# Two token tiles of the feed-forward input gated and quantised during the last state-space step, and the last batch's expert slots computed after its first shared column

## The chip, the cores and the metric

The kernel runs on one core of a Trainium2 chip. TensorE (PE) does matrix products and transposes into PSUM banks, VectorE (DVE), ScalarE (ACT) and GpSimd (POOL) do elementwise work, and the SyncE queue (SP) issues most transfers. Each engine takes its own instructions in order and waits on semaphores for the others. The metric is the device time of one execution in microseconds, as the median of several runs.

## The reference, cut to what matters

Four sequences of 512 tokens with 512 channels pass through two layers. Layer 0 is a gated linear attention and a mixture of experts (16 experts, 6 chosen for each token, 2 shared). Layer 1 is a state-space mixer (four chunks of 128 tokens in this kernel) and a feed-forward block whose inputs are quantised in blocks of 32. Each of the four blocks reads the running sum through a sigmoid gate and a ratio tensor that hang on the condition.

```python
# _bi_wkv, the gate in front of each block
base = sigmoid(r) * (num / maximum(den, 1e-08))
# state-space mixer, its last steps
Y = Y + x_heads * D_param[:, None]
Y = Y.reshape(Bsz, L, D_INNER) * silu(z)
return rmsnorm(Y) @ fq4(W_out).T
# feed-forward
def _mx_dequant(t):
    blocks = t.reshape(rows, feat // 32, 32)
    scales = maximum(max(abs(blocks)) / 448.0, 1e-30)
    q = (blocks / scales).astype(float8_e4m3fn).astype(float32)
    return (q * scales).reshape(rows, feat)
gate = _mx_dequant(x2d) @ _mx_dequant(gate_w).T
up = _mx_dequant(x2d) @ _mx_dequant(up_w).T
out = _mx_dequant(silu(gate) * up) @ _mx_dequant(down_w).T
# the whole
x = x + L0_attn(L0_cond(x, ...)); x = x + L0_ffn(L0_cond2(x, ...))
x = x + L1_attn(L1_cond(x, ...)); x = x + L1_ffn(L1_cond2(x, ...))
```

## The kernel before

The program has three parts, one after the other. **Layer 0's first part** (0 to about 1262 us) takes the four batches `b` in turn: attention, then `route_and_share`. There PE computes the router's logits and then six shared columns `j` (`ST = 6`): a gate and an up product of 512 columns (L927), and the down product of the column before (L914), each four products (eight records in a trace). DVE ranks the experts in `route`, sends the mask by `m_mask`, then multiplies gate and up of each column (L2021, `m_prod`). At `j == 1` PE makes the prefix sums over the mask (L932, L933, `m_pref`), and after column `j == 2` DVE turns them into slots (`place`, L1944 to L1955, `m_slot`); in the last batch it goes on with `tile_tables` (the expert tiles' tables, `e_tab`) and `pads(0)`, `pads(1)`. On `m_slot` POOL writes the token numbers to their slots with 24 indirect transfers (L1587, `ids_put`). When the last batch's have landed, SP (`first_tiles`, L635) loads the first tiles' token numbers and expert weights, POOL gathers their rows (L1599), and PE starts the **expert tiles** with `expert_x(0)` (L964), which also needs `x1b`, the sum over the shared columns that DVE makes after the last of them (L2038).

**The expert tiles** (63 of 256 slots, to about 2320 us) are followed by **layer 1**, four batches of about 430 us. A batch has projections (L1080), four state-space steps `k` and 16 feed-forward steps `i` (four blocks `ib` of 512 hidden channels by four token tiles `t`).

A state-space step goes: PE broadcasts decays (L1090), DVE subtracts (`differences`, L2225), ACT exponentiates (L1509), DVE masks (`masked`, L2231), PE multiplies (`diagonal`, L1099) and reads the state (L1157, `s_yo`), DVE sums up y (L2259 to L2270, `s_y`), ACT takes its root mean square (L1531, L1533, `s_yss`), DVE the reciprocal (L2281, `s_yr`), ACT scales (`normalise`, L1513), PE transposes (L1107), ACT copies out (L1518), and PE projects in two halves (`out_project`, L1121, `s_out`). Step `k` holds the projection of tile `k - 1`; the last tile's stands behind the loop. DVE adds a projected tile to the running sum (`residual_tile`, L2217, `x3_ready`), and in the last step it does so for tile 2 before it waits for `s_yss`.

Behind the last projection come, for each token tile, ACT's sigmoid (L1538, `sig3`), DVE's product with the ratio R[3] (L2288, `h_tile`), PE's transpose to bank 7 (`x_transpose`, L1180, `f_tx`), DVE's quantisation (`quantise_x`, L1656 to L1666 and L2296 to L2302, `f_qx`), PE's transpose back (`xq_transpose`, L1191, `f_tq`) and ACT's copy to `xqT` (L1543, `f_xT`). Then step `i` can begin: a gate product (L1226), an up product (L1232, `f_gu`), ACT's silu (L1548), DVE's product (L2310, `f_mul`) and quantisation, PE's transposes (L1206) and, once a block, the down products (L1213). Tiles 0 and 1 are quantised ahead of the loop and tiles 2 and 3 inside of it, after DVE's steps 0 and 1. DVE's part in the order before:

```python
dve.reciprocal(ss[:, 2:3], ss[:, 1:2]).then_inc(s_yr.sem, 1)
for k in range(NT):
    if k == NT - 1:
        residual_tile(k)
    ...                      # wait for sig3, h = sigmoid * R[3], h_tile
quantise_x(0)
quantise_x(1)
for i in range(FB * NT):
    ...                      # product, quantise; after i = 0, 1: quantise_x(i + 2)
```

For the next batch POOL gathers expert outputs (`collect(b + 1)`, L1609) from `f_vx` of tile 0 on, and DVE weighs them (`weigh`, L2109, L2111) from step 5 on.

## Time and profile before

| | |
|---|---|
| median of 3 runs | 4135.53 us (4132.06 to 4138.08) |
| the profiled execution | 4128.88 us, of which its span 4127.0 us |
| PE busy | 3569.0 us (86%) |
| DVE busy | 2611.4 us (63%) |
| ACT busy | 1194.5 us (29%) |
| POOL busy | 522.4 us (13%) |
| TensorE clock, mean granted share | 0.917 |
| shares of the chain that ended last | PE 62%, DVE 23%, DVE's sequencer 5%, ACT 4%, DMA 2% |

The page of the profile gives the busy time of each engine, the span in 40 slices, the chain of work that ended last and the costliest groups. A timeline lists instructions in order of time; a stretch table gives the busy time of each engine and the granted clock of a stretch. In a group of records a matmul of 32-bit data counts twice. A bracket behind a row tells how long the engine had been idle before it, and what released it.

### The profile page before, as it was taken

How to read it: one execution, taken by the hardware profiler on the slowest of the kernel's cores; microseconds unless marked ns; L12 is line 12 of the kernel's file. 1: busy time of each engine (PE TensorE's matmuls, PEld its weight loads, DVE VectorE, ACT ScalarE, POOL GpSimd, SP SyncE). 2: the span in 40 equal slices, each digit the busy share in tenths (PEclk: the TensorE clock that was granted, in tenths of full speed). 3: DMA queues.
4: the chain of work that ended last, by engine and by line, in shares of the span. 5: the costliest groups of instructions: out<-in, count | busy, mean ns of one | idle time of the engine just before them, and what ended most of it. 6: DMA issues, size and time to landing. Idle time of an engine off the chain costs nothing.

```text
span 4127.0 us, 38866 instructions
## 1 busy us (share of the span) xinstructions
PE 3569.0 (86%) x13526; PEld 2231.7 (54%) x13526; DVE 2611.4 (63%) x3722; ACT 1194.5 (29%) x1974; POOL 522.4 (13%) x419
## 2 busy tenths in 40 slices
PE   1887877887887999999999959898989898989898
PEld 1553643644545777777777625543554356434643
DVE  5877887877863656778777344564356444744463
ACT  1332332432322444333333222222221222113210
POOL 1002003003012111111111022020112011101100
PEclk9889989888898999999999978899789988998899
DMA  3212212202205777777777430132013201130011
GB/s 140 69 32 58 60 31 63 71 18 50 63 13 188 241 244 228 241 234 241 246 226 239 161 143 31 72 107 82 31 72 107 82 31 70 66 121 35 9 53 41
DMA packets 277843, 444.62 MB, mean 108 GB/s; under 512 B 52560, under 2 KB 189776, under 8 KB 265104
## 3 DMA queue, kind: packets, MB, share of 16 engines
q1 hardware_dynamic: 256768, 383.74, 28.2%
q0 software_dynamic: 20880, 58.40, 4.4%
q8 instruction: 108, 1.77, 0.2%
q14 instruction: 87, 0.71, 0.1%
HBM read 368.49 MB, written 97.70 MB: 113 GB/s over the span
## 4 chain that ended last, share of the span: by engine, by line
PE 62%; DVE 23%; DVEq 5%; ACT 4%; DMA 2%; issue 2%; POOL 1%; SPq 0%; ACTq 0%; POOLq 0%
PE bank L969 14%; PE bank L980 7%; PE bank L1213 6%; PE bank L1226 4%; PE bank L1232 4%; PE bank L787 3%; PE bank L1121 3%; PE bank L1080 3%; DVE sb_gla L1797 2%; DVE sb_ratio L1772 2%; PE bank L1099 2%; DVEq L1778 2%; PE bank L767 2%; PE bank L1157 1%; PE bank L1090 1%
## 5 line engine op out<-in xcount | busy, mean ns | idle before, releaser
L969 PE MATMUL bank<-sb_xT,sb_work 128*128 128x256 f32 x3024 | 665.2, 380 | 1.6 <-issue 0.8
L969 PEld LDWEIGHTS bank<-sb_xT,sb_work 128*128 128x128 f32 x3024 | 574.8, 191 | 100.0 <-issue 24.6
L787 PE MATMUL bank<-sb_gla,sb_work 128*128 128x256 f32 x896 | 260.4, 443 | 113.0 <-DVE sb_work L1799 100.2
L980 PE MATMUL bank<-sb_work,sb_hT 128*128 128x512 f32 x756 | 334.7, 592 | 0.0
L787 PEld LDWEIGHTS bank<-sb_gla,sb_work 128*128 128x128 f32 x896 | 188.9, 218 | 175.9 <-DVE sb_work L1799 121.6
L767 PE MATMUL bank<-sb_hT,sb_work 128*128 128x512 f32 x384 | 183.3, 626 | 99.4 <-DVE sb_hT L1746 99.4
L1599 POOL DMA_INDIRECT sb_parts<-scratch_h,sb_small x126 | 139.0, 1103 | 915.4 <-DMA sb_small<-scratch_ids 895.8
L1226 PE MATMUL bank<-sb_parts,sb_small 128*128 128x512 f32 x512 | 244.3, 622 | 4.5 <-ACT sb_small L1543 4.5
L1232 PE MATMUL bank<-sb_parts,sb_small 128*128 128x512 f32 x512 | 230.8, 593 | 5.9 <-DVE sb_work L2310 5.9
L1213 PE MATMUL bank<-sb_work,sb_parts 128*128 128x512 f32 x512 | 230.2, 609 | 2.7 <-ACT sb_work L1554 2.7
L1080 PE MATMUL bank<-sb_parts,sb_hT 128*128 128x512 f32 x512 | 228.7, 605 | 0.0
L1797 DVE TENSOR_TENSOR sb_gla<-sb_gla,sb_work 128x1024 f32<-128x1024 f32 x112 | 145.1, 1296 | 129.7 <-PE bank L787 123.8
L980 PEld LDWEIGHTS bank<-sb_work,sb_hT 128*128 128x128 f32 x756 | 138.9, 190 | 151.2 <-issue 151.1
L927 PE MATMUL bank<-sb_work,sb_parts 128*128 128x512 f32 x384 | 178.9, 622 | 37.4 <-ACT sb_small L1399 27.0
L1587 POOL DMA_INDIRECT scratch_ids<-sb_small x96 | 106.6, 1110 | 553.0 <-DVE sb_small L1955 525.0
L2225 DVE TENSOR_TENSOR sb_work<-bank,sb_work 128x512 f32<-128x512 f32 x64 | 44.1, 689 | 208.7 <-PE bank L1090 134.8
L767 PEld LDWEIGHTS bank<-sb_hT,sb_work 128*128 128x128 f32 x384 | 76.1, 203 | 183.4 <-DVE sb_hT L1746 101.9
L1232 PEld LDWEIGHTS bank<-sb_parts,sb_small 128*128 128x128 f32 x512 | 96.8, 190 | 130.5 <-issue 119.6
L1080 PEld LDWEIGHTS bank<-sb_parts,sb_hT 128*128 128x128 f32 x512 | 98.0, 193 | 127.1 <-issue 122.6
L2310 DVE TENSOR_TENSOR sb_work<-sb_work,bank 128x512 f32<-128x512 f32 x64 | 43.8, 685 | 192.7 <-PE bank L1232 192.7
L1213 PEld LDWEIGHTS bank<-sb_work,sb_parts 128*128 128x128 f32 x512 | 99.0, 196 | 123.6 <-issue 119.2
L1226 PEld LDWEIGHTS bank<-sb_parts,sb_small 128*128 128x128 f32 x512 | 98.2, 201 | 113.8 <-issue 113.8
(363 smaller groups left out, 5978.6 us busy)
## 6 DMA issues: line engine op xcount, KB each, us to landing
sb_work<-scratch_gu SPq DMA_DIRECT2D x63, 1408.0 KB, 7.5
sb_parts<-scratch_mx SPq DMA_DIRECT2D x16, 3072.0 KB, 10.2
sb_work<-moe_w SPq DMA_DIRECT2D x63, 512.0 KB, 5.6
scratch_y<-sb_work SPq DMA_DIRECT2D x63, 512.0 KB, 6.9
sb_parts<-scratch_fq SPq DMA_DIRECT2D x24, 1024.0 KB, 7.9
sb_work<-w_qkvg SPq DMA_DIRECT2D x64, 256.0 KB, 2.6
scratch_gu<-moe_w SPq DMA_DIRECT2D x32, 512.0 KB, 5.7
sb_parts<-fT SPq DMA_DIRECT2D x48, 256.0 KB, 3.0
```

The costliest lines, as they stand in the source:

```text
L767: mm = pe.matmul(dst, gw[:, m, k, :], ch(hT, k), start=(k == 0), stop=(k == NC - 1))
L787: mm = pe.matmul(dst.rearrange("p (h n l) -> p h n l", h=HPC, l=size), kS[u % 2][:, k * P:(k + 1) * P], late[:, :, k, :, 1, :], start=True ...
L927: mm = pe.matmul(bank(4 + which), shw[j][:, a:a + P], ch(h1, k), start=(k == 0), stop=(k == NC - 1))
L969: mm = pe.matmul(dst, egu[j % 3][:, which * NC + k, m * P:(m + 1) * P], xt[j % 2][:, k, :], start=(k == 0), stop=(k == NC - 1))
L980: mm = pe.matmul(bank(YB[s]), einter[j % 2][:, m * SLOTS + s * P:m * SLOTS + (s + 1) * P], edn[j % 3][:, m * D:(m + 1) * D], start=(m == 0 ...
L1080: mm = pe.matmul(bank(6 + i % 2), ch(hT, kk)[:, k * P:(k + 1) * P], wzx[:, m, kk, :], start=(kk == 0), stop=(kk == NC - 1))
L1121: mm = pe.matmul(bank(7)[:, oc * P:(oc + 1) * P], wout[:, i // 4, i % 4, oc * P:(oc + 1) * P], ynT8[:, i, k * P:(k + 1) * P], start=(i == ...
L1213: mm = pe.matmul(bank(oc), fw[ib % 2][:, 2, i, oc * P:(oc + 1) * P], hqT[ib % 2][:, i, :], start=(ib == 0 and i == 0), stop=(ib == FB - 1 ...
L1226: mm = pe.matmul(bank(4), xqT[:, k, t * P:(t + 1) * P], fw[ib % 2][:, 0, k, :], start=(k == 0), stop=(k == NC - 1))
L1232: mm = pe.matmul(bank(5), xqT[:, k, t * P:(t + 1) * P], fw[ib % 2][:, 1, k, :], start=(k == 0), stop=(k == NC - 1))
L1599: pool.indirect_dma_start(hg[j % 2][:, s, :], None, d_h, bass.IndirectOffsetOnAxis(ap=idx[j % 4][:, s:s + 1], axis=0))\
L1797: tt(late, late, now2[:, :, 0].unsqueeze(1).unsqueeze(3).to_broadcast([P, HPC, n, size]), ALU.mult)
```

## The change

It has two parts. In every batch of layer 1, tiles 0 and 1 of the feed-forward input no longer stand behind the last projection. ACT takes their sigmoids (`sigmoid3`) and DVE gates them (`gate3`) in the last state-space step; PE transposes them to banks 4 and 5 after that step's last `diagonal`, ahead of the second half of tile 2's projection. DVE quantises both after the reciprocal of the last step, ahead of the gate of tile 2, the last tile's residual and the gate of tile 3. `xq_transpose(0)` stands between the halves of the last projection. The first up product waits for `f_vx` of tile 1 (bank 5). The buffers `fqx`, `fxv`, `fxm`, `fxamx` and `xqT` lie in `sb_gla`, and POOL's `collect(b + 1)` waits for `s_out` of the last tile. Nothing is computed more or less often.

In the last batch of layer 0, PE's prefix sums stand behind the gate and up product of column 0, and `place`, `tile_tables`, `pads(0)` and `pads(1)` behind DVE's product of column 0.

```diff
--- before.py
+++ after.py
@@ -487,17 +487,15 @@
 
 
         fw = [big[:, s * 6144:(s + 1) * 6144].rearrange("p (m c o) -> p m c o", m=3, c=4) for s in range(2)]
-        xqT = small2[:, 0:NC * T].rearrange("p (c t) -> p c t", c=NC)
+        xqT = gla[:, 0:NC * T].rearrange("p (c t) -> p c t", c=NC)
         fs = [w(2048 + s * 512, 512) for s in range(2)]
         fh = w(3072, 512)
         fv = w(3584, 512)
         fm = w(4096, 512)
         fq = [w(4608 + s * 512, 512) for s in range(2)]
         hqT = [w(5632 + s * 2048, 2048).rearrange("p (i t) -> p i t", i=4) for s in range(2)]
-        fqx = [w(9856 + s * 512, 512) for s in range(2)]
-        fxv = [w(10944 + s * 512, 512) for s in range(2)]
-        fxm = [w(11968 + s * 512, 512) for s in range(2)]
-        fxamx = [w(12992 + s * 64, 64) for s in range(2)]
+        fqx, fxv, fxm = [[gla[:, a + s * 512:a + (s + 1) * 512] for s in range(2)] for a in (2048, 3072, 4096)]
+        fxamx = [gla[:, 5120 + s * 64:5184 + s * 64] for s in range(2)]
         famx = w(9728, 64)
 
 
@@ -927,7 +925,7 @@
                             mm = pe.matmul(bank(4 + which), shw[j][:, a:a + P], ch(h1, k),
                                            start=(k == 0), stop=(k == NC - 1))
                         mm.then_inc(event.sem, 1)
-                    if j == 1:
+                    if j == (0 if b == NB - 1 else 1):
                         pe.wait_ge(m_mask.sem, m_mask.at(b, 1))
                         pe.matmul(bank(7)[:, 64:128], cst("tri"), rk[:, 448:512], start=True, stop=True)
                         pe.matmul(bank(7)[:, 128:192], cst("ones"), rk[:, 448:512], start=True, stop=True)\
@@ -1083,6 +1081,28 @@
                 pe.wait_ge(s_silu.sem, s_silu.at(b, NT * 4))
                 pe.wait_ge(s_gm.sem, s_gm.at(b, 1))
 
+                def x_transpose(t, dst=7):
+
+                    pe.wait_ge(h_tile.sem, h_tile.at(b, t + 1))
+                    if t == 2:
+                        pe.wait_ge(x3_ready.sem, x3_ready.at(b, NT))
+                    if t == 3:
+                        pe.wait_ge(f_vx.sem, f_vx.at(b, t))
+                    for c in range(NC):
+                        mm = pe.transpose(bank(dst)[:, c * P:(c + 1) * P], ch(hT, c)[:, t * P:(t + 1) * P], idn)
+                    mm.then_inc(f_tx.sem, 1)
+
+                def xq_transpose(t):
+
+                    pe.wait_ge(f_qx.sem, f_qx.at(b, t + 1))
+                    if t == 1:
+                        pe.wait_ge(f_xT.sem, f_xT.at(b, 1))
+                    elif t > 1:
+                        pe.wait_ge(f_hT.sem, f_hT.at(b, t - 1))
+                    for c in range(NC):
+                        mm = pe.transpose(bank(6)[:, c * P:(c + 1) * P], fqx[t % 2][:, c * P:(c + 1) * P], idn)
+                    mm.then_inc(f_tq.sem, 1)
+
                 def cs_bcast(k, g):
 
                     for hh in range(4):
@@ -1158,6 +1178,9 @@
                                        start=True, stop=True)
                     mm.then_inc(s_yo.sem, 1)
                     diagonal(k, 3)
+                    if k == NT - 1:
+                        for i in range(2):
+                            x_transpose(i, 4 + i)
                     if k < NT - 1:
                         pe.wait_ge(s_xdec.sem, s_xdec.at(b, k + 1))
                         for h in range(2):
@@ -1169,32 +1192,8 @@
                 pe.wait_ge(s_y.sem, s_y.at(b, NT))
                 y_transposes(NT - 1)
                 out_project(NT - 1, 0)
+                xq_transpose(0)
                 out_project(NT - 1, 1)
-
-                def x_transpose(t):
-
-                    pe.wait_ge(h_tile.sem, h_tile.at(b, t + 1))
-                    if t:
-                        pe.wait_ge(f_vx.sem, f_vx.at(b, t))
-                    for c in range(NC):
-                        mm = pe.transpose(bank(7)[:, c * P:(c + 1) * P], ch(hT, c)[:, t * P:(t + 1) * P], idn)
-                    mm.then_inc(f_tx.sem, 1)
-
...
-                pe.wait_ge(x3_ready.sem, x3_ready.at(b, NT))
-                x_transpose(0)
-                xq_transpose(0)
-                x_transpose(1)
 
                 def f_transposes(i):
                     pe.wait_ge(f_q.sem, f_q.at(b, i + 1))
@@ -1228,6 +1227,8 @@
                         mm.then_inc(f_gate.sem, 1)
                         if i:
                             pe.wait_ge(f_mul.sem, f_mul.at(b, i))
+                        else:
+                            pe.wait_ge(f_vx.sem, f_vx.at(b, 2))
                         for k in range(NC):
                             mm = pe.matmul(bank(5), xqT[:, k, t * P:(t + 1) * P], fw[ib % 2][:, 1, k, :],
                                            start=(k == 0), stop=(k == NC - 1))
@@ -1512,6 +1513,10 @@
                     act.wait_ge(s_yr.sem, s_yr.at(b, k + 1))
                     act.activation(Yt[k % 2], Yt[k % 2], ACT.Copy, scale=ss[:, 2:3]).then_inc(s_yn.sem, 1)
 
+                def sigmoid3(k):
+                    act.wait_ge(x3_ready.sem, x3_ready.at(b, k + 1))
+                    act.activation(tile_of(hT, k), tile_of(X2[b % 2], k), ACT.Sigmoid).then_inc(sig3.sem, 1)
+
                 def y_evacuate(k):
                     act.wait_ge(s_tr.sem, s_tr.at(b, k + 1))
                     for i in range(2):
@@ -1527,20 +1532,22 @@
                     decay_exp(k, 1)
                     decay_exp(k, 2)
                     decay_exp(k, 3)
+                    if k == NT - 1:
+                        for t in range(2):
+                            sigmoid3(t)
                     act.wait_ge(s_y.sem, s_y.at(b, k + 1))
                     act.activation(Dx, Yt[k % 2], ACT.Square, accum_out=ss[:, 0:1])
                     act.drain()
                     act.activation(ss[:, 1:2], ss[:, 0:1], ACT.Sqrt, bias=eps_rms, scale=1.0 / DI).then_inc(s_yss.sem, 1)
                 normalise(NT - 1)
                 y_evacuate(NT - 1)
-                for k in range(NT):
-                    act.wait_ge(x3_ready.sem, x3_ready.at(b, k + 1))
-                    act.activation(tile_of(hT, k), tile_of(X2[b % 2], k), ACT.Sigmoid).then_inc(sig3.sem, 1)
-
+                sigmoid3(2)
                 for i in range(FB * NT + 1):
                     if i < NT:
                         act.wait_ge(f_tq.sem, f_tq.at(b, i + 1))
                         act.activation(xqT[:, :, i * P:(i + 1) * P], r3(bank(6), P), ACT.Copy).then_inc(f_xT.sem, 1)
+                    if i == 0:
+                        sigmoid3(NT - 1)
                     if i < FB * NT:
                         act.wait_ge(f_gate.sem, f_gate.at(b, i + 1))
                         if i >= 2:
@@ -1638,7 +1645,7 @@
 
 
                 if b + 1 < NB:
-                    pool.wait_ge(f_vx.sem, f_vx.at(b, 1))
+                    pool.wait_ge(s_out.sem, s_out.at(b, NT))
                     collect(b + 1)
 
 
@@ -2019,7 +2026,7 @@
                     if j >= 2:
                         dve.wait_ge(m_down.sem, m_down.at(b, j - 1))
                     tt(inter[j % 2], sgt[j % 2], bank(5), ALU.mult).then_inc(m_prod.sem, 1)
-                    if j == 2:
+                    if j == (0 if last else 2):
                         place(b)
                         if last:
                             tile_tables()
@@ -2211,6 +2218,13 @@
                     .then_inc(s_gm.sem, 1)
                 dve.wait_ge(s_exps.sem, s_exps.at(b, 1))
 
+                def gate3(k):
+
+                    if k == 0:
+                        dve.wait_ge(ld_r3.sem, 16 * (b + 1))
+                    dve.wait_ge(sig3.sem, sig3.at(b, k + 1))
+                    tt(tile_of(hT, k), tile_of(hT, k), tile_of(R[3], k), ALU.mult).then_inc(h_tile.sem, 1)
+
                 def residual_tile(k):
 
                     dve.wait_ge(s_out.sem, s_out.at(b, k + 1))
@@ -2252,6 +2266,10 @@
                     differences(3)
                     masked(2)
                     masked(3)
+                    if k == NT - 1:
+                        for t in range(2):
+                            gate3(t)
+                        dve.drain()
 
                     y = Yt[k % 2]
                     dve.wait_ge(s_yo.sem, s_yo.at(b, k + 1))
@@ -2279,19 +2297,10 @@
                         residual_tile(k - 1)
                 dve.wait_ge(s_yss.sem, s_yss.at(b, NT))
                 dve.reciprocal(ss[:, 2:3], ss[:, 1:2]).then_inc(s_yr.sem, 1)
-                for k in range(NT):
-                    if k == NT - 1:
-                        residual_tile(k)
-                    if k == 0:
-                        dve.wait_ge(ld_r3.sem, 16 * (b + 1))
-                    dve.wait_ge(sig3.sem, sig3.at(b, k + 1))
-                    tt(tile_of(hT, k), tile_of(hT, k), tile_of(R[3], k), ALU.mult).then_inc(h_tile.sem, 1)
-                dve.drain()
-
-                def quantise_x(t):
+                def quantise_x(t, src=7):
                     dve.wait_ge(f_tx.sem, f_tx.at(b, t + 1))
                     v, m = fxv[t % 2], fxm[t % 2]
-                    quantise_head(bank(7), v, m, fxamx[t % 2])
+                    quantise_head(bank(src), v, m, fxamx[t % 2])
                     dve.drain()
                     tt(v, v, m, ALU.add).then_inc(f_vx.sem, 1)
                     dve.drain()
@@ -2302,8 +2311,12 @@
                     tt(r3(fqx[t % 2], QB), r3(v, QB), bcast(fxamx[t % 2][:, 16:32], QB), ALU.mult)\
                         .then_inc(f_qx.sem, 1)
 
-                quantise_x(0)
-                quantise_x(1)
+                quantise_x(0, 4)
+                quantise_x(1, 5)
+                gate3(2)
+                residual_tile(NT - 1)
+                gate3(NT - 1)
+                dve.drain()
                 for i in range(FB * NT):
                     dve.wait_ge(f_silu.sem, f_silu.at(b, i + 1))
                     dve.wait_ge(f_gu.sem, f_gu.at(b, i + 1))
```

## Rows read from the trace of the kernel before

**Rows 1.** Stretches: length, busy us (records) by engine, clock, DMA share, GB/s

```profile
1500.00:1600.00 100.00, 100.00 (x431) 75.44 (x429) 61.23 (x80) 42.25 (x81) 13.49 (x12) 1.00 0.72 233
...
2700.00:2800.00 100.00, 94.35 (x255) 43.57 (x254) 65.03 (x111) 19.14 (x25) 21.09 (x18) 1.00 0.32 111
```

**Rows 2.** The same view: in the last state-space step of batch 0

```profile
2604.00:2608.00 4.00, 4.00 (x7) 1.46 (x6) 0.20 (x1) 0.00 (x0) 0.00 (x0) 0.50 0.00 0
```

**Rows 3.** Timeline of batch 0's last state-space step: start, us, engine, line, operation

```profile
2601.68 1.47 DVE L2231 SCALAR_TENSOR_TENSOR sb_work<-sb_work 128x512 f32<-128x512 f32 x2
...
2607.80 1.29 DVE L2259 TENSOR_TENSOR sb_work<-bank,sb_small 128x512 f32<-128x512 f32 x2 [4.65 <-PE bank L1157]
...
2609.46 4.73 PE L1121 MATMUL bank<-sb_work,sb_parts 128*128 128x128 f32 x25
...
2613.08 1.06 ACT L1531 ACTIVATE sb_work<-sb_work 128x1024 f32<-128x1024 f32 x1 [10.66 <-DVE sb_work L2270]
...
2615.00 0.69 DVE L2217 TENSOR_TENSOR sb_ratio<-sb_ratio,bank 128x512 f32<-128x512 f32 x1 [1.95 <-PE bank L1121]
...
2616.19 0.16 DVE L2281 RECIPROCAL sb_small<-sb_small 128x1 f32<-128x1 f32 x1 [0.49 <-ACT sb_small L1533]
...
2619.91 9.01 PE L1121 MATMUL bank<-sb_work,sb_parts 128*128 128x128 f32 x64 [1.17 <-ACT sb_work L1518]
```

**Rows 4.** The same timeline: sigmoids, then the start of the feed-forward

```profile
2619.88 1.28 ACT L1538 ACT_TABLE_LOAD   x1
...
2621.17 1.67 ACT L1538 ACTIVATE sb_hT<-sb_ratio 128x512 f32<-128x512 f32 x3
...
2631.13 0.69 DVE L1656 TENSOR_REDUCE sb_work<-bank 128x16 f32<-128x512 f32 x1
...
2635.79 0.69 DVE L2302 TENSOR_TENSOR sb_work<-sb_work 128x512 f32<-128x512 f32 x1
...
2638.43 4.62 PE L1226 MATMUL bank<-sb_parts,sb_small 128*128 128x512 f32 x8
...
2646.32 0.60 PE L1191 MATMUL bank<-sb_const,sb_work 128*128 128x128 f32 x4
...
2646.59 0.69 DVE L2310 TENSOR_TENSOR sb_work<-sb_work,bank 128x512 f32<-128x512 f32 x1 [2.40 <-PE bank L1232]
...
2660.10 5.73 PE L1226 MATMUL bank<-sb_parts,sb_small 128*128 128x512 f32 x8
```

**Rows 5.** Groups by line, all four batches: shapes, count, busy and mean, idle before

```profile
L1191 PE MATMUL bank<-sb_const,sb_work 128*128 128x128 f32 x64 | 13.6, 350 | 40.2 <-DVE sb_work L2302 37.9 <-ACT sb_work L1554 2.3
```

**Rows 6.** Timeline: POOL's gathers for the next batch's rows

```profile
2700.74 1.41 POOL L1609 DMA_INDIRECT sb_work<-scratch_y,sb_small  x1 [57.86 <-DVE sb_work L2109]
```

**Rows 7.** Timeline of the last batch's shared columns and the first expert tile

```profile
1196.33 0.20 DVE L1909 TENSOR_SCALAR sb_work<-sb_work 128x64 f32<-128x64 f32 x1
...
1201.35 0.69 DVE L2021 TENSOR_TENSOR sb_small<-sb_small,bank 128x512 f32<-128x512 f32 x1
...
1211.33 7.03 PE L927 MATMUL bank<-sb_work,sb_parts 128*128 128x512 f32 x16
...
1219.06 0.17 DVE L1944 TENSOR_TENSOR sb_work<-bank,sb_small 128x16 f32<-128x16 f32 x1
...
1222.75 1.01 POOL L1587 DMA_INDIRECT scratch_ids<-sb_small  x1 [127.85 <-DVE sb_small L1955]
...
1237.86 0.63 DVE L2021 TENSOR_TENSOR sb_small<-sb_small,bank 128x512 f32<-128x512 f32 x1
...
1238.54 3.70 PE L927 MATMUL bank<-sb_work,sb_parts 128*128 128x512 f32 x8 [3.02 <-DVE sb_small L2021]
...
1259.44 2.48 DVE L2038 TENSOR_TENSOR sb_work<-sb_work,bank 128x512 f32<-128x512 f32 x4 [6.12 <-PE bank L914]
...
1281.81 1.94 PE L964 MATMUL bank<-sb_const,sb_parts 128*128 128x128 f32 x8 [22.40 <-DMA sb_parts<-scratch_h,sb_small]
```

**Rows 8.** The chain that ended last, in order of time: the last scatter landing

```profile
1255.37 13.72 DMA scratch_ids<-sb_small
```

9 lines of the change are left out of this document (removed).

## The prediction

> **What bounds the kernel now.** I read the stretches first. In the expert tiles PE is busy for the whole of a stretch, in the feed-forward steps for 94% of it, at full clock both [rows 1]. So what is saved ahead of either stretch should last to the end, and what matters is how early each of them starts. Then I read timelines at those two starts.
>
> At the feed-forward's start (batch 0) PE ends the last projection at 2619.91 + 9.01 = 2628.92 [rows 3] and starts the first gate product at 2638.43 [rows 4]: 9.5 us in which it does only transposes. Between them run, in one chain, the last residual, tile 3's gate, x_transpose(0), DVE's quantisation of tile 0 (2631.13 to 2635.79 + 0.69 = 2636.48, so 5.35 us), xq_transpose(0) and ACT's copy. The clock falls to its lower level (1.2 GHz) on the way: the first gate product takes 4.62 us and the one at 2660.10, behind another wait for DVE, 5.73 us, against 3.5 us at full clock (7.03 for two such groups [rows 7]). All four batches do the same: PE's idle time in front of L1191, released by DVE's L2302, is 37.9 us in all, 9.5 a batch [rows 5].
>
> At the expert tiles' start PE idles 22.40 us until the first tile's rows have come [rows 7]. That chain is: DVE's product of column 2, `place` from 1219.06, POOL's scatters from 1222.75, the last issued at 1255.37 and landed 13.72 us later [rows 8], SP's load of the token numbers, POOL's gather, PE at 1281.81 [rows 7].
>
> **Part one, feed-forward input, batch 0.** I follow each engine in its new order.
>
> *Sigmoids and gates, tiles 0 and 1.* ACT is free from 2613.08 - 10.66 = 2602.42 [rows 3]. A table load is 1.28 us, and three sigmoids take 1.67, so 0.56 each [rows 4]: done at about 2604.9. DVE is out of `masked` at 2601.68 + 1.47 = 2603.15 and waits 4.65 us for the state product until 2607.80 [rows 3]. Two gates of about 0.69 fit behind the sigmoids and end near 2606, with 1.8 us to spare: cost 0. Were that cover gone, each would put 0.69 us on the path. ACT's next work is at 2613.08, so the table load is hidden as well. R[3] is no new wait: the copy that is needed was loaded at the batch's start.
>
> *Two transposes on PE.* They stand behind the last `diagonal`, about 2609.5, and the gates are done by then. Each is four records, 0.60 us at full clock [rows 4] and up to twice that at half; the clock here is 0.50 [rows 2]. So 1.0 to 2.1 us, I take 1.6. `diagonal` is ahead of them, so y isn't touched. Behind them on PE is tile 2's second projection half (from 2609.46), and on DVE `residual_tile(2)` (2615.00) waits for that, with the reciprocal (2616.19) queued behind the residual [rows 3]. The residual goes to 2616.60, ends at 2617.29, and the reciprocal comes at 2617.35: 1.2 us later on the path (0.6 to 1.7). The slack that takes the rest is the 0.49 us that DVE waited there.
>
> *Quantisation.* It begins right behind the reciprocal, at 2617.5, and ends at 2622.9 for tile 0 and 2628.3 for tile 1 (5.35 each). Normalising, transposing, copying and the first half of the last projection run beside it: they took from 2616.19 to 2619.91 + 4.5 = 2624.4, now to 2625.6. So xq_transpose(0) finds its input 2.7 us early; it puts 0.6 to 1.1 us in front of the second half (0.85 taken). ACT's copy hides beside that half.
>
> *The last projection* ends at 2628.92 + 1.2 + 0.85 = 2631.0, and the gate and up products follow with nothing between: 7.0 us, so DVE's first product comes at 2638.1 where it came at 2646.59 [rows 4]. The bank-5 wait ended by 2628.3. Tile 2's gate fits before 2631.0; the last residual and tile 3's gate end near 2633.5, in front of DVE's first product and behind nothing that needs it. This is **8.5 us earlier**. From there the order is as it was: step 0, tile 2, step 1, tile 3 on DVE, with the same waits of PE for tiles 2 and 3. The saving is not more, since these two quantisations are still at DVE's pace, and not less, since every later instruction follows from that product. Bounds: 1.2 may be 0.6 or 1.7, 0.85 may be 0.6 or 1.1, and the first gate product may still be at the lower clock (1.1 us more): 7 to 9.5 us a batch.
>
> *Who else is moved.* POOL's gathers wait for `s_out`, 2631.0, instead of `f_vx`, which came just ahead of DVE's last operation at 2635.79 [rows 4]: 4 us earlier, where the steps are 8.5 us earlier. They have room, as POOL later waits 57.86 us for DVE's weighing and not the other way round [rows 6]. SP loads the second weights behind the same `s_out`, 2 us later than now, for block 1 that starts some 40 us on. Moving buffers costs nothing.
>
> Four batches: 4 x 8.5 = **34 us** (28 to 38).
>
> **Part two, the last batch's slots.** The mask is out at 1196.53 and DVE's first product starts at 1201.35, ready when PE has made up(0), so PE's prefix sums don't wait. `place` starts behind that product at about 1202.1 instead of 1219.06 [rows 7]: **17.0 us** earlier, and so are 24 scatters, the landing, SP's load and the gather, if DMA gives the same. Rows come at 1264.8 instead of 1281.8.
>
> The price is that `place`, the tables and two pads hold DVE for 1237.86 - 1219.06 = 18.8 us, now ahead of the product of column 1. Behind it PE waits with up(2). Gate(2) starts at 1211.33 as now and ends at 1214.8; DVE's product comes at 1202.1 + 18.8 to 1221.6: PE idles 6.9 us, where now it idles 3.02 at column 4 [rows 7]. Twelve groups of 3.5 follow (up, down and three columns, then the last down): 42 us, end at 1263.6. If the clock falls, the first group takes 5.73 as at 2660.10 [rows 4], 2.2 more: 1265.8. The 3.02 us wait was followed by a group of 3.70, so a fall isn't certain; I take it, since this wait is twice as long. DVE's sums, 2.48 us, end at 1268.3 [rows 7]. Now that, and not the rows, lets PE start: late next is the shared columns. 1281.81 - 1268.4 = 13.4 us. With a shorter idle time before it the first expert tile may run at the higher clock from its start, 0 to 2.5 us; I take 1. **14.4 us** (11 to 18). It carries on, as the expert tiles are PE's.
>
> **Sum.** 34 + 14.4 = 48.4 us. The profiled execution took 4128.88, its span 4127.0: it would come to 4080.5. The median shown is 6.65 above that execution, and I keep this distance: 4135.5 - 48.4 = **4087.1**.
>
> **Rivals.**
>
> *The early start doesn't carry.* Steps 5 to 13 also hold the weighing for the next batch, and if rows or loads set their pace, three of four savings vanish at `collect`. 8.5 + 14.4 = 23 us, **4112.6**. For it: the gathers gain 4 us and the steps 8.5. Against: [rows 6].
>
> *Shared columns eat the slots' gain.* If the wait of 6.9 us leaves the clock low for several groups (2.2 each), the shared columns' end moves on: six such groups put the start back to 1281.6. Then 34 us stay, **4101**. Against: behind the slow group of 4.62 us the next was at full clock at once (2638.43 + 4.62 + 3.5 = 2646.55, and DVE's product starts at 2646.59 [rows 4]).
>
> *Slower: the clock stays low in the first feed-forward steps.* A group takes 3.5 us at the higher level and about 6.9 at the lower. In the first steps PE still waits for DVE's tiles 2 and 3. If that held PE at the lower level for the eight groups of steps 0 to 3 (28 us at full clock) it would cost 27 us more, less the 3.3 that two groups lose now: 24. It turns the part into a loss from 2.5 such groups a batch on. 4 x (24 - 8.5) - 14.4 = +48 us: **4183**. Against: now the longer gap, 9.5 us, costs only 1.1 us behind it, and the change closes it. For it stands a rule of the Trainium skill (TensorE: Matmul & The Clock Gate, "What's actually happening"): the slow clock is the default and activity releases it, and the page's caveats add that a clock has been seen stuck low for over 50 us. The groups of 4.62 and 5.73 us agree with the first; no row here shows the second.
>
> *It doesn't do what it says.* If the two quantisations push something on the path, above all `residual_tile(3)` behind them (they end at 2628.3, the projection at 2631.0), the chain only changes its order. That needs them 2.7 us later; with 10 us more the first part is worth nothing and 4121 is left; without the second part too, 4135.
>
> **Chances.** Forecast (4076 to 4102) 0.78; no carrying 0.07; shared columns 0.05; slower 0.03; less than it says 0.07, about half of it within 0.2%. 0.2% (8 us) is about what a measurement of this kernel can tell from no change. Faster by more: 0.78 + 0.07 + 0.05 + 0.03 = 0.93; same 0.04; slower 0.03. Bounds of the sum: 28 + 11 = 39 us and 38 + 18 = 56 us, so 4079.5 to 4096.5; the runs spread by 3 each way, and the two partial rivals reach 4101 and 4112.6. I give 4072 to 4109.
>
> **What would show it.** In the new trace: first gate product right behind the last projection (gap under 0.5 us, now 9.5); DVE's L2302 no releaser of the first L1191; the reciprocal 1 to 2 us later after L2217; DVE's product L2310 8.5 us nearer to the end of `masked`; the group at 2660.10 still slow behind its wait. At the experts: `place` right behind the first product, one wait of about 7 us at up(2), first expert transpose 13 to 14 us earlier, released by DVE's L2038 and not by the gather. Wrong would be: PE waiting in the middle of the last projection for f_qx, steps 5 to 13 with new waits for gathers, or scatters that land no sooner.

## The result, and the profile of the changed kernel

The changed kernel takes 4084.01 us (median of 4 runs, 4081.36 to 4089.35) and the kernel before, measured beside it, 4133.8 (4 runs, 4128.31 to 4138.08): a ratio of 0.9881 [0.9867, 0.9895]. The forecast was 4087.1. The profiled execution took 4081.36 us, against 4128.88 before.

The page of the changed kernel: span, then busy time of each engine.

```profile
span 4079.5 us, 38866 instructions
PE 3568.3 (87%) x13526; PEld 2237.0 (55%) x13526; DVE 2608.3 (64%) x3722; ACT 1199.7 (29%) x1978; POOL 523.3 (13%) x419
```

The span is 47.5 us shorter. PE is busy for as long as before (3568.3 us, then 3569.0); what went is idle time, at the two places below.

**Start of the feed-forward, batch 0.** Timeline of the changed kernel: start, us, engine, line, operation, and in brackets the idle time before it with its releaser. Its lines answer [rows 3, 4].

```profile
2591.02 3.78 PE L1177 MATMUL bank<-sb_work,sb_small 64*128 64x512 f32 x4
...
2596.49 1.92 PE L1092 MATMUL bank<-sb_const,sb_hT 128*128 128x128 f32 x8
...
2598.20 4.82 PE L1141 MATMUL bank<-sb_work,sb_parts 128*128 128x128 f32 x32
...
2603.06 0.69 DVE L2231 TENSOR_TENSOR sb_ratio<-sb_ratio,bank 128x512 f32<-128x512 f32 x1 [2.97 <-PE bank L1141]
2603.66 0.16 DVE L2299 RECIPROCAL sb_small<-sb_small 128x1 f32<-128x1 f32 x1
...
2607.39 5.41 PE L1141 MATMUL bank<-sb_work,sb_parts 128*128 128x128 f32 x32 [1.18 <-ACT sb_work L1523]
...
2612.64 0.60 PE L1103 MATMUL bank<-sb_const,sb_gla 128*128 128x128 f32 x4
...
2613.07 3.74 PE L1141 MATMUL bank<-sb_work,sb_parts 128*128 128x128 f32 x32
...
2616.65 3.60 PE L1225 MATMUL bank<-sb_parts,sb_gla 128*128 128x512 f32 x8
...
2620.08 3.60 PE L1233 MATMUL bank<-sb_parts,sb_gla 128*128 128x512 f32 x8
...
2623.79 0.69 DVE L2323 TENSOR_TENSOR sb_work<-sb_work,bank 128x512 f32<-128x512 f32 x1 [4.86 <-PE bank L1233]
```

L1177 is the last state read, L1092 the two `x_transpose`, L1103 `xq_transpose(0)`, L1141 the output projection, L1225 and L1233 the gate and up products. On DVE L2231 is a residual, L2299 the reciprocal and L2323 the first product of the steps. The projection ends at 2613.07 + 3.74 = 2616.81 and the first gate product stands right behind it: the 9.5 us of [rows 3, 4] are gone, and the product takes 3.60 us where it took 4.62. The traces say the same of every batch: 9.51 us from the projection's end to the first gate product in each of the four before, nothing in each of the four now.

The groups by line, all four batches: count, busy us, mean ns, then idle time before them by releaser. The last answers [rows 5].

```profile
L1225 PE MATMUL bank<-sb_parts,sb_gla 128*128 128x512 f32 x512 | 239.1, 611 | 4.5 <-ACT sb_gla L1548 3.5 <-issue 1.0
L1233 PE MATMUL bank<-sb_parts,sb_gla 128*128 128x512 f32 x512 | 230.8, 593 | 6.6 <-DVE sb_work L2323 6.6
...
L1212 PE MATMUL bank<-sb_work,sb_parts 128*128 128x512 f32 x512 | 230.3, 609 | 2.7 <-ACT sb_work L1561 2.7
...
L1103 PE MATMUL bank<-sb_const,sb_gla 128*128 128x128 f32 x64 | 11.8, 315 | 15.4 <-DVE sb_gla L2311 12.3 <-ACT sb_work L1561 3.1
```

PE's wait for a quantised tile fell from 37.9 us to 12.3. Before, it was 6.18 us for tile 0 and 2.97 for tile 2 in every batch, and 1.26 for tile 3 in the last; now it is tile 2's alone, 2.97 to 3.32 a batch. In all steps of all batches the gate, up and down products are idle for 13.8 us together, 12.8 of it for ACT and DVE: no gather or load sets the pace of a step.

**Shared columns and the start of the experts.** The same view; its lines answer [rows 7]. L925 and L912 are the products of the shared columns, L962 the first expert transpose; on DVE L2028 is `m_prod`, L1951 the first of `place` and L2045 the sums over the shared columns.

```profile
1176.90 7.01 PE L899 MATMUL bank<-sb_small,sb_work 128*128 128x16 f32 x32 [5.91 <-DVE sb_work L1873]
...
1198.54 0.69 DVE L2028 TENSOR_TENSOR sb_small<-sb_small,bank 128x512 f32<-128x512 f32 x1
1199.15 0.17 DVE L1951 TENSOR_TENSOR sb_work<-bank,sb_small 128x16 f32<-128x16 f32 x1
...
1217.96 0.63 DVE L2028 TENSOR_TENSOR sb_small<-sb_small,bank 128x512 f32<-128x512 f32 x1
...
1218.64 5.10 PE L925 MATMUL bank<-sb_work,sb_parts 128*128 128x512 f32 x8 [8.21 <-DVE sb_small L2028]
...
1261.54 2.48 DVE L2045 TENSOR_TENSOR sb_work<-sb_work,bank 128x512 f32<-128x512 f32 x4 [6.12 <-PE bank L912]
1264.08 1.10 PE L962 MATMUL bank<-sb_const,sb_parts 128*128 128x128 f32 x8 [2.57 <-DVE sb_work L2045]
```

`place` (L1951) stands right behind the first product, the block of `place` and the tables holds DVE for 1217.96 - 1199.15 = 18.8 us, PE waits 8.21 us for it, and the first expert transpose is released by DVE's sums after 2.57 us, not by the rows after 22.40. The executions differ in where they stand by then, so I count from the router's logits (L899 here, at 1179.70 before): the transpose comes 1264.08 - 1176.90 = 87.18 us behind them, and came 1281.81 - 1179.70 = 102.11 behind. That is 14.9 us.

**Where the rest stands.** For each batch, from the timelines: us from the last state read to the first gate product, and to the first down product.

| batch | to gate, before | after | to down, before | after | saved |
|---|---|---|---|---|---|
| 0 | 34.44 | 25.63 | 89.88 | 80.05 | 9.8 |
| 1 | 34.20 | 25.53 | 90.08 | 79.93 | 10.2 |
| 2 | 34.19 | 25.32 | 89.88 | 79.87 | 10.0 |
| 3 | 32.57 | 25.37 | 88.37 | 79.75 | 8.6 |

So 38.6 us in the feed-forward, 14.9 at the experts' start, 1.2 in the first expert tile (its second transpose comes 13.97 us behind the first, before 15.20), and 2.8 that this execution was ahead at the logits, where nothing was changed: 57.5. The span gave 47.5. Of the 10.0 us difference 7.4 stand between the first and the last state read of batches 0 and 1 (93.21 and 96.32 us, before 88.95 and 93.20), ahead of what the change touches; in the repeat below they take 89.19 and 93.37, so most of it is the execution and not the kernel. The last section shows the clock there.

### The profile page after: what moved, and what is told of

Same layout as the page of the kernel before. It is cut to its first block, busy times and chain, and to the rows that moved or that the text cites. A ratio compares the mean times of both kernels' runs of the same rounds, so it can differ in the third digit from the quotient of the medians.

```text
span 4079.5 us, 38866 instructions
## 1 busy us (share of the span) xinstructions
PE 3568.3 (87%) x13526; PEld 2237.0 (55%) x13526; DVE 2608.3 (64%) x3722; ACT 1199.7 (29%) x1978; POOL 523.3 (13%) x419
## 4 chain that ended last, share of the span: by engine, by line
PE 55%; DVE 8%; ACT 2%; DVEq 2%; issue 1%; DMA 1%; ACTq 0%; POOL 0%; POOLq 0%
PE bank L967 14%; PE bank L978 7%; PE bank L1212 6%; PE bank L1225 4%; PE bank L1233 4%; PE bank L1141 4%; PE bank L1078 3%; PE bank L1119 2%; PE bank L1177 1%; PE bank L1110 1%; PE bank L962 1%; PE bank L1040 1%; PE bank L987 1%; PE bank L1152 1%; DVE sb_work L2118 1%
## 5 line engine op out<-in xcount | busy, mean ns | idle before, releaser
L1225 PE MATMUL bank<-sb_parts,sb_gla 128*128 128x512 f32 x512 | 239.1, 611 | 4.5 <-ACT sb_gla L1548 3.5
L1233 PE MATMUL bank<-sb_parts,sb_gla 128*128 128x512 f32 x512 | 230.8, 593 | 6.6 <-DVE sb_work L2323 6.6
L1212 PE MATMUL bank<-sb_work,sb_parts 128*128 128x512 f32 x512 | 230.3, 609 | 2.7 <-ACT sb_work L1561 2.7
L925 PE MATMUL bank<-sb_work,sb_parts 128*128 128x512 f32 x384 | 179.0, 622 | 42.4 <-ACT sb_small L1400 27.2
L2323 DVE TENSOR_TENSOR sb_work<-sb_work,bank 128x512 f32<-128x512 f32 x64 | 43.8, 685 | 200.6 <-PE bank L1233 200.6
L1233 PEld LDWEIGHTS bank<-sb_parts,sb_gla 128*128 128x128 f32 x512 | 96.8, 190 | 131.2 <-issue 119.6
L1212 PEld LDWEIGHTS bank<-sb_work,sb_parts 128*128 128x128 f32 x512 | 98.9, 196 | 123.8 <-issue 119.4
L1225 PEld LDWEIGHTS bank<-sb_parts,sb_gla 128*128 128x128 f32 x512 | 96.3, 196 | 109.7 <-issue 109.7
```

Of the source, the lines that this page charges most:

```text
L925: mm = pe.matmul(bank(4 + which), shw[j][:, a:a + P], ch(h1, k), start=(k == 0), stop=(k == NC - 1))
L1212: mm = pe.matmul(bank(oc), fw[ib % 2][:, 2, i, oc * P:(oc + 1) * P], hqT[ib % 2][:, i, :], start=(ib == 0 and i == 0), stop=(ib == FB - 1 ...
L1225: mm = pe.matmul(bank(4), xqT[:, k, t * P:(t + 1) * P], fw[ib % 2][:, 0, k, :], start=(k == 0), stop=(k == NC - 1))
L1233: mm = pe.matmul(bank(5), xqT[:, k, t * P:(t + 1) * P], fw[ib % 2][:, 1, k, :], start=(k == 0), stop=(k == NC - 1))
```

## The experiments

**One part at a time, and twice more early.** `e1_ffn_only` is the changed kernel with the last batch's slots as before:

```diff
-                    if j == (0 if b == NB - 1 else 1):
+                    if j == 1:
...
-                    if j == (0 if last else 2):
+                    if j == 2:
```

> Only the feed-forward part; the last batch's prefix sums and slots stand behind column 1 and 2 as before. My theory: the two parts are independent and add up. The feed-forward part alone takes 34 us by the prediction and 38 us by the trace of the changed kernel (from the last state read to the first down products 79.95 us a batch on average, before 89.55), so 34 to 38 us faster than before, ratio 0.9908 to 0.9918. The first expert transpose starts near 1282 as before, 22 us of PE idle in front of it. Rival (the early start doesn't carry): only the last batch gains, 8 to 10 us, ratio 0.998. Rival (the parts share a gain): under 30 us.

Measured: 4105.12 us, ratio 0.9905 [0.9891, 0.992]. The first expert transpose comes 102.10 us behind the logits, as before, PE idles 22.39 us in front of it, and the down products 80.44, 79.67, 79.87 and 79.75 us behind the state read, as in the changed kernel.

`e2_slots_only` is the kernel before with the same two conditions turned the other way.

> Only the last batch's slots behind its first column, layer 1 as before. My theory: 14 to 16 us faster than before, ratio 0.9961 to 0.9966; PE idles about 8 us at the up product of column 2, the first expert transpose comes about 15 us earlier against the logits than before and is released by DVE's sums over the shared columns, not by the gathered rows. Rival (the shared columns eat it): the shared columns end so much later that the start is near its old place, under 5 us.

Measured: 4127.06 us, 0.996 [0.9946, 0.9974]. Its timeline at the slots:

```profile
1182.15 7.01 PE L901 MATMUL bank<-sb_small,sb_work 128*128 128x16 f32 x32 [5.91 <-DVE sb_work L1866]
...
1223.90 6.54 PE L927 MATMUL bank<-sb_work,sb_parts 128*128 128x512 f32 x8 [6.53 <-DVE sb_small L2021]
...
1270.79 1.97 PE L964 MATMUL bank<-sb_const,sb_parts 128*128 128x128 f32 x8 [2.57 <-DVE sb_work L2038]
```

The start is 88.64 us behind the logits, 13.5 earlier than before, with a wait of 6.53 us. I had expected 15 us and a wait of 8, as in the first trace of the changed kernel. The feed-forward still shows its gap of 9.51 us. The two parts add up: 0.9905 x 0.996 = 0.9865, beside 0.9881 and 0.9859 for both together.

`e3_three_tiles` takes tile 2 into the early stretch as well, so that its wait in step 1 should go:

```diff
...
 xq_transpose(0)
+x_transpose(2, 0)
 out_project(NT - 1, 1)
...
-if i + 2 < NT:
-    x_transpose(i + 2)
+if i == 0:
+    x_transpose(3)
...
 quantise_x(0, 4)
-quantise_x(1, 5)
 gate3(2)
+quantise_x(1, 5)
 residual_tile(NT - 1)
+quantise_x(2, 0)
 gate3(NT - 1)
...
-if i + 2 < NT:
-    quantise_x(i + 2)
+if i == 0:
+    quantise_x(3)
```

> The changed kernel with tile 2 moved as well: PE transposes it to bank 0 between the halves of the last projection, DVE quantises it after the last residual and ahead of the feed-forward loop, tile 3 after step 0. Theory: what is left at the feed-forward's start is DVE's pace. PE waits 2.98 us for tile 2's quantisation and again for tile 3's, with the lower clock behind the first wait. DVE idles about 8 us between the quantisation of tile 1 and its first product, room for 5.35 us. So the wait of 2.98 us goes, the later one shrinks, and a batch gains 3 to 4 us: 12 to 16 us faster than the changed kernel, ratio to before 0.984 to 0.985. Rival: DVE is so full in steps 0 to 3 that PE waits as long in another place (for f_q or f_mul): under 1 us a batch, ratio as the changed kernel's 0.988. Rival (slower): the third quantisation delays tile 3's gate and DVE's first product by over 1 us a batch, 4 us slower than the changed kernel.

Measured: 4066.03 us, 0.9814 [0.9799, 0.9829]. The down products come 75.11, 75.9, 75.75 and 75.33 us behind the state read: 4.4 a batch sooner than in the changed kernel, 17.5 in all, and more than the 3 to 4 a batch that I had expected. At the same place of the steps the timeline now reads:

```profile
2642.81 0.63 PE L1101 MATMUL bank<-sb_const,sb_gla 128*128 128x128 f32 x4 [0.78 <-ACT sb_work L1560]
...
2644.22 3.67 PE L1224 MATMUL bank<-sb_parts,sb_gla 128*128 128x512 f32 x8 [0.78 <-ACT sb_gla L1547]
```

where the changed kernel had

```profile
2635.42 1.12 PE L1103 MATMUL bank<-sb_const,sb_gla 128*128 128x128 f32 x4 [2.98 <-DVE sb_gla L2311]
...
2637.31 5.72 PE L1225 MATMUL bank<-sb_parts,sb_gla 128*128 128x512 f32 x8
```

A wait of 2.98 us and the slow group behind it (5.72 against 3.67) cost more than the wait alone; what is left is ACT's copies, 0.78 us each.

`e4_split_tables` is the changed kernel with only `place` behind the first product; the tables and pads stay behind column 2:

```diff
                     if j == (0 if last else 2):
                         place(b)
+                    if j == 2:
                         if last:
                             tile_tables()
```

> The changed kernel, but of what stood behind column 0 only the slots (3.4 us of DVE) stay there; the tables and the two pads (15.4 us) stand behind column 2. Theory: in the changed kernel the shared columns and not the rows are late at the expert tiles' start (PE waits 2.57 us for DVE's sums there). With the block split PE's wait of 8.2 us at column 2 goes, the shared columns end some 9 us earlier, and the gathered rows become what is late: the start moves by about 2.5 us, 2 to 3 us faster than the changed kernel, ratio to before about 0.9875. Rival: the scatters and the rows come later as well, since the tables, loads of SP and POOL share DMA and ports: no gain. Rival: the start follows the shared columns wholly, 8 us.

Measured: 4086.72 us, 0.9852 [0.9839, 0.9864].

```profile
1186.18 7.01 PE L899 MATMUL bank<-sb_small,sb_work 128*128 128x16 f32 x32 [5.91 <-DVE sb_work L1873]
...
1272.00 1.94 PE L962 MATMUL bank<-sb_const,sb_parts 128*128 128x128 f32 x8 [9.39 <-DMA sb_parts<-scratch_h,sb_small]
```

PE no longer waits at column 2, so the shared columns end sooner, and now the rows are late again, by 9.39 us. Still the start is 85.82 us behind the logits: 2.8 sooner than in the execution of the changed kernel that comes next, 1.4 sooner than in the first. Three more executions with this split, below, show 84.64 to 85.66; e2, e3, e5, e6 and e7, without it, show 88.62 to 88.87. So the traces give it about 3 us, which is under what the times can tell (0.9852 beside 0.9859 of the repeat). The rival that the tables hold up the rows finds no support: SP loads the token numbers 73.6 to 75.0 us behind the logits with the split, and 73.0 to 74.9 without it.

**The same kernel again.** `e5_after_again` is the changed kernel, unchanged.

> The changed kernel itself, once more, so that the variants of this call have it beside them on the same chip, and to see which stretches of layer 1 vary between two executions of one program. Expected: ratio to before 0.987 to 0.989; 79.4 to 80.1 us from the last state read to the first down products in each batch; in steps 0 to 2, where the changed kernel's first trace had steps of 30.4 and 35.3 us beside 32.0 and 30.6, different ones are the slow ones, if it is the clock, and the same ones, if it is the change.

Measured: 4083.33 us, 0.9859 [0.9837, 0.9882], a little under the expected 0.987 to 0.989.

```profile
1180.94 7.00 PE L899 MATMUL bank<-sb_small,sb_work 128*128 128x16 f32 x32 [5.91 <-DVE sb_work L1873]
...
1222.67 6.55 PE L925 MATMUL bank<-sb_work,sb_parts 128*128 128x512 f32 x8 [6.52 <-DVE sb_small L2028]
...
1269.56 1.97 PE L962 MATMUL bank<-sb_const,sb_parts 128*128 128x128 f32 x8 [2.57 <-DVE sb_work L2045]
```

Here the wait is 6.52 us, the start 88.62 behind the logits, and the first tile gives nothing (15.12). The length of the wait doesn't set the start: e3 waited 8.23 us and started at 88.87. What sets the first execution apart is the group behind the wait, 5.10 us there and 6.5 to 6.8 in the others. This execution sums up better: 36.9 us in the feed-forward (82.01, 79.75, 79.86 and 79.72 to the down products) and 13.5 at the experts, less 1.2 that it was behind at the logits, are 49.2, and its span of 4079.7 is 47.3 shorter. The 82.01 of batch 0, outside the 79.4 to 80.1 that I had expected, is a second wait: PE stands 2.85 us for tile 3's quantisation, in one of the eight batches of the two executions.

**Where the transposes cost.** `e6_transposes_later` puts the two transposes behind tile 2's projection instead of ahead of it:

```diff
                     diagonal(k, 3)
-                    if k == NT - 1:
-                        for i in range(2):
-                            x_transpose(i, 4 + i)
...
                     if k:
                         out_project(k - 1, 1)
+                    if k == NT - 1:
+                        for i in range(2):
+                            x_transpose(i, 4 + i)
```

> The changed kernel with x_transpose(0) and x_transpose(1) behind the second half of tile 2's projection, not ahead of it. My step: ahead of it they delay that half, the residual of tile 2 and with it the reciprocal, by 1.2 us a batch on the path. So a batch gets 0.8 to 1.2 us shorter from the last state read to the first gate product, 3 to 5 us in all, and the reciprocal follows ACT's root with the 0.5 us it had in the kernel before. Rival: the transposes fill a gap and keep the clock up; then nothing changes (within 0.3 us a batch).

Measured: 4092.59 us, 0.9873 [0.9851, 0.9895]: by the time it can't be told from the kernel with the transposes ahead (0.9859 [0.9837, 0.9882]). The timelines do: 24.97, 24.96, 24.96 and 24.97 us from the state read to the gate product, against 24.93 to 25.63 in eight batches of the changed kernel, 25.35 in the mean. So the place costs 0.4 us a batch up to the first gate product, where I had expected 0.8 to 1.2, and nothing of it is left behind: to the down products it is 79.41, 80.64, 79.71 and 80.33 us, 80.0 in the mean, beside 79.9 and 80.3 in the two executions of the changed kernel.

**Which of the moves does it.** `e7_quantise_behind` leaves sigmoids, gates and transposes early and puts both quantisations back behind the last residual, and `xq_transpose(0)` behind the projection; ACT's last sigmoid goes ahead of the steps with them:

```diff
...
 out_project(NT - 1, 0)
-xq_transpose(0)
 out_project(NT - 1, 1)
+xq_transpose(0)
...
 sigmoid3(2)
+sigmoid3(NT - 1)
...
-    if i == 0:
-        sigmoid3(NT - 1)
...
-quantise_x(0, 4)
-quantise_x(1, 5)
 gate3(2)
 residual_tile(NT - 1)
 gate3(NT - 1)
 dve.drain()
+quantise_x(0, 4)
+quantise_x(1, 5)
```

> The changed kernel with sigmoids, gates and transposes of tiles 0 and 1 early, but both quantisations behind the last residual and tile 3's gate, as before, and xq_transpose(0) behind the last projection. My theory: the gain is the quantisation's 5.35 us beside the projection and the closed gap, not the early gates. So the gap between the last projection and the first gate product comes back at 8 to 9.5 us, with the slow first group behind it, and 7 to 9 us a batch of the part's gain are lost: 28 to 36 us slower than the changed kernel, ratio to before 0.995 to 0.997. Rival: the early gates and transposes are worth half of it; then a gap of about 5 us and 16 to 20 us slower than the changed kernel.

Measured: 4138.83 us, 0.9988 [0.9975, 1.0002].

```profile
2610.96 10.36 PE L1141 MATMUL bank<-sb_work,sb_parts 128*128 128x128 f32 x64 [1.18 <-ACT sb_work L1523]
2628.94 1.12 PE L1103 MATMUL bank<-sb_const,sb_gla 128*128 128x128 f32 x4 [7.62 <-DVE sb_gla L2310]
2630.84 5.37 PE L1225 MATMUL bank<-sb_parts,sb_gla 128*128 128x512 f32 x8 [0.78 <-ACT sb_gla L1549]
```

The gap is back (9.5 us from 2621.3 to 2630.84) and the first gate product is slow again. The gap is 9.51 us in all four batches, to the hundredth what it was before. Down products come 93.28, 91.23, 91.52 and 92.76 us behind the state read, 12.3 a batch or 49 us later than in the changed kernel, and even later than before. I had expected a loss of 28 to 36 us. All of the feed-forward's gain is lost, so the moved sigmoids, gates and transposes are worth nothing by themselves; what makes the gain is that DVE quantises beside the projection. This order is another 1.2 to 4.4 us a batch worse than before, and the traces show where: the projection ends 26.28, 25.07, 25.30 and 26.14 us behind the state read (before 24.93, 24.69, 24.69 and 23.06), and PE waits 1.25 to 1.67 us for tile 3, where before it did so in the last batch alone, for 1.26. In batch 0 the two halves of the last projection take 10.36 us against 9.01, at a granted clock of 0.69 against 0.82, and the first gate product 5.37 against 4.62. Why the clock is lower there stays open, and with it a part of my miss.

**Versions that beat both kernels.** `e8_combined` is the changed kernel with the edits of e3, e4 and e6; `e9_two_variants` has those of e3 and e4; `e10_combined_again` is e8's kernel once more, beside e9.

> All three variants on the changed kernel: three tiles quantised ahead of the loop, the tables behind column 2, and the two transposes behind tile 2's second half. If they are independent: 16 us from the third tile (4 x 4.2 in the trace), 1.5 to 3 us from the tables, 3 to 4 us from the transposes, 21 to 23 us faster than the changed kernel, ratio to before about 0.983 where the changed kernel has 0.988. Rival: the transposes' gain vanishes, since DVE then starts its first quantisation earlier but the third one is what it is late with: 18 us.

> The changed kernel with three tiles quantised ahead of the loop and the tables behind column 2, the transposes where the changed kernel has them. Traces so far: the third tile takes 4 to 5 us a batch from the stretch between the last state read and the first down products, the tables 2.6 to 4 us from the start of the expert tiles, the later transposes 0.4 us a batch. If that adds up, a profiled execution near 4058 to 4062 and a ratio to before of 0.982 or 0.983, within 2 us of the kernel with all three. Rival (the wider intervals hide a loss in layer 1 that the stretches measured so far don't hold, say in the steps behind the first down products): ratio above 0.985.

> The kernel with all three variants once more, since its interval was wide (0.9809 to 0.9857). Expected: 0.982 to 0.983, beside the kernel with two variants at most 2 us faster. Rival: 0.985 or more, no faster than the changed kernel.

| | us | ratio to before | to down, mean of 4 | logits to expert start |
|---|---|---|---|---|
| e8 | 4074.98 | 0.9833 [0.9809, 0.9857] | 75.10 | 84.64 |
| e9 | 4063.63 | 0.9811 [0.9791, 0.9832] | 75.85 | 85.66 |
| e10 | 4061.03 | 0.9803 [0.9786, 0.9821] | 75.56 | 84.92 |

Their medians are 9 to 23 us under the changed kernel's. The intervals of e9 and e10 lie clear of its two, and their ratios are a little under the 0.982 to 0.983 that I had expected; e8's executions run from 4056.84 to 4081.33 us and its interval reaches into that of the repeat (0.9837 to 0.9882), although it is e10's kernel. That the third tile does nearly all of it follows from e3 alone (0.9814). e3, e9 and e10 don't differ by more than the measurement.

## Why the prediction was right, point by point

**What bounds the kernel.** Right: an earlier start of the feed-forward or of the experts stays to the end. e1 and e2 show each alone, and that they add up. The last expert tiles end 2366.03 - 2347.03 = 19.0 us earlier in the changed kernel (14.9 + 1.2 + 2.8 = 18.9).

**The feed-forward: mechanism right, term too small.** 34 us were forecast, with bounds of 28 and 38, and 38.6 measured (36.9 in the repeat); three of the four batches lie above the bound of 9.5. In batch 0, where 8.5 were forecast and 9.8 measured, 1.2 of the 1.3 is one step: the projection's end was put 2.05 us later against the state read, and it is 0.9 later (25.79 us, before 24.93).
- *Reciprocal, 1.2 us later (0.6 to 1.7):* it is 0.44 later (2603.66 - 2591.02 = 12.64 us behind the state read, before 12.20). The two transposes take what was forecast, 2598.20 - 2596.49 = 1.7 us against 1.6. But the projection's half behind them takes 4.82 us where it took 5.51 ([rows 3] shows only the first 25 records of that half; the whole of it is the row below), since a part of the slow stretch falls on the transposes (granted clock 0.50 from 2595 to 2598 us, 0.75 from 2598 to 2603; before, 0.58 from 2608 to 2614); the residual comes 1.0 us later and not 1.6, and the slack of 0.49 us in front of the reciprocal takes half of that. The forecast had carried the half over at its old length, and the result lies below its bounds, as the next one does. e6 agrees from the other side: with the transposes moved away there are 0.4 us to be had, and the half takes 5.41 us again.

```profile
2609.46 5.51 PE L1121 MATMUL bank<-sb_work,sb_parts 128*128 128x128 f32 x32
```

- *xq_transpose(0), 0.85 us (0.6 to 1.1):* 0.41. The second half of the last projection ends 9.42 us behind the start of the first, before 9.01. The group's row shows 0.60 us, but groups overlap by some 0.15 us at their ends, which a row of one group doesn't tell.
- *Sigmoids and gates at cost 0*, *quantisation in time:* right. Behind the gates DVE still waits 1.86 us for the state read (1.8 to spare forecast). Tile 0 is quantised at 2609.07 and its transpose runs at 2612.64, 3.6 us later (2.7 forecast).
- *First gate product at full clock:* right, 3.60 us.
- *What is late next, tiles 2 and 3:* right for tile 2, 2.98 us and a slow group of 5.72 behind it; e3 shows what that costs. For tile 3 PE waits for DVE in one of eight batches (2.85 us, in the repeat), as before in one of four.
- *The reading of [rows 5]:* wrong, without harm to the sum. The 37.9 us are not four gaps of 9.5: they are 6.18 us for tile 0, inside the gap, 2.97 for tile 2 behind it, and once 1.26 for tile 3. That the gap was 9.51 us in each batch is true by the timelines.

**The slots.** `place` starts 22.25 us behind the logits, before 39.36: 17.1 us earlier (17.0 forecast), the block takes 18.8 as forecast, and the scatters give a little more: SP loads the token numbers 73.0 us behind the logits, before 91.1, so 18.1 us earlier (16.2 to 17.0 in e2, e3, e5, e6 and e7). The wait at up(2) was put at 6.9 us; it is 6.5 in e2 and in the repeat, and 8.21 in the first execution, where the first gate and up product took 7.13 us against 8.83 and PE came to the wait sooner. The fall of the clock behind it was put at 2.2 us more than full speed's 3.5; the group took 6.54, 6.55 and 5.10. Late next is the shared columns, as forecast, released by DVE's sums. The start was forecast 13.4 us earlier; it is 14.9, 13.5 and 13.5. e3, e6 and e7, with the same slots, give 13.2 to 13.5 too, so the first execution is the odd one. The 1 us for a warm first tile was there in the first execution (1.2) and not in the repeat (0.1).

**The sum** of 48.4 us is nearer to the measured 49.8 (4133.8 - 4084.0) than its terms are to theirs, and that is in part luck: the traces of the two executions give 54.7 and 50.4 at the two places, and stages that the change leaves alone differ by several us from one execution to the next. The medians don't tell the size closer either. Beside e5 the kernel before stood at 4144.24 us (16 runs, 4133.07 to 4155.06), 60.9 above the changed kernel's 4083.33. That the change is faster is clear in both measurements; whether it is worth 50 us or 60 is not.

**The rivals.** *Doesn't carry:* fell. L1225, L1233 and L1212 wait for no gather, and all four batches save alike. *Shared columns eat the gain:* the wait is there, but one group behind it is slow and the next takes 3.60. (Its sum counted a slow group twice: five more behind the one in the forecast would have put the start at 1279.4, not 1281.6.) *Slower, the clock stays low:* the first two groups of the steps take 3.60 us each. The Trainium skill (TensorE: Matmul & The Clock Gate, "What's actually happening") says that the slow clock is the default and activity releases it. The traces agree in that direction: 5.10, 6.54 and 5.72 us behind waits, 3.60 behind busy stretches; but 3.70 behind the wait of 3.02 us before, so not every wait is followed by a fall. Of the clock that stays low for over 50 us, of which the page's caveats tell, the traces show only an idle form: from 2351.3 to 2402.5 us the changed kernel is granted 0.50, and PE is busy for 7.4 us of it. With PE busy no run here shows one. *It doesn't do what it says:* fell, since the gap is gone; e7 shows that the gap would have stayed with DVE's quantisations behind the residual.

## What to carry to other kernels

Where PE stands idle between two stretches, look for elementwise work there that needs nothing of the first stretch's end: put beside that stretch it cost nothing here, and moving its producers early without it was worth nothing. Where an order written out by hand moves a block ahead, what it costs is read behind it on the same in-order engine, and splitting the block or taking one more tile along tells who is late next; here one more tile gave 4.4 us a batch. And cost an inserted group with the group that follows it: here 1.7 us of transposes made what follows 1.0 us later, since the group behind them got shorter.

## What was not expected of the hardware

Which state-space steps run at the lower level differs between executions of one and the same kernel. The windows view of one step of batch 1, in the changed kernel and in its repeat: length, busy us (records) of PE, its weight loads, DVE, ACT and POOL, granted clock, DMA share and GB/s.

```profile
2949.00:2984.00 35.00, 33.18 (x153) 24.43 (x152) 16.32 (x21) 8.65 (x12) 8.01 (x4) 0.70 0.00 1
```

```profile
2953.00:2984.00 31.00, 29.18 (x154) 20.51 (x154) 16.32 (x21) 8.65 (x12) 8.01 (x4) 0.83 0.00 1
```

DVE, ACT and POOL are busy for the same time, PE for 4 us more, at a clock of 0.70 against 0.83. From state read to state read the same steps take 35.25 and 30.70 us (35.24 again in e6), and the first step of batch 0 takes 31.96 and 27.83. The other way round, the first step of batch 1 takes 30.44 and 31.96. What makes a step fall on one side or the other no run here shows. Over the two batches it comes to 7 us: a single trace can hide or feign as much in stages that nobody changed. For a change of this size the two places are to be measured from a mark just ahead of each, in more than one execution; the span alone would have credited or charged the change with them.
